# Queries' and keys' stacks of high and low parts: laid out by SBUF-to-SBUF transfers in place of selection products and copies, with the slots of the schedule redone

## What is computed

```python
Q = (x_text @ Wq).reshape(B, T, 4, 32);  K = (x_vision @ Wk).reshape(B, G, 4, 32)
scores = einsum('bthd,bghd->bhtg', Q, K) / sqrt(32)        # masked by vision_mask
topv, topi = top_k(scores, 32);  probs = softmax(topv)
attn_mean = scatter(probs at topi).mean(over heads);  c_t = (attn_mean @ V)
# then: layernorm(x), FiLM by c_t, an S4D filter along T, FiLM, residual, FFN (gelu),
# layernorm, gated residual; a router picks 1 of 8 experts (swiglu) plus a shared expert
```

## Time and profile before

| | us |
|---|---|
| median of 3 runs | 1884.37 (1880.43 to 1888.39) |
| profiled execution | 1881.66 |
| its span on the core | 1879.9 |
| busy in the span: DVE | 1573.5 (84%) |
| PE | 1437.8 (76%) |
| POOL | 1206.7 (64%) |
| ACT | 1112.8 (59%) |
| mean granted TensorE clock | 0.857 of full |

### The profile page before, as it was taken

How to read it: one execution, slowest core, us unless ns; L and a number is a source line. 1 busy time by engine, 2 the same in 40 slices (tenths; PEclk the granted TensorE clock), 3 DMA queues, 4 the chain that set the end, 5 groups by cost and what they waited for, 6 DMA issues and landing times. The chain is left out here.

```text
span 1879.9 us, 21018 instructions
## 1 busy us (share of the span) xinstructions
PE 1437.8 (76%) x6493; PEld 1025.5 (55%) x6493; DVE 1573.5 (84%) x2300; ACT 1112.8 (59%) x2257; POOL 1206.7 (64%) x1325
## 2 busy tenths in 40 slices
PE   4631445767986798779988988897989787887897
PEld 2321324535654565455756565655665666656696
DVE  6899999999999989998999999999999999101321
ACT  3575664476648654865597658765876576233342
POOL 1496873766676657667767875887588747733422
PEclk9665667888897788878999998999989897998999
DMA  7000000000100010002311320122022202652322
GB/s 225 18 4 14 3 16 2 27 12 12 26 25 12 12 40 21 3 12 76 90 51 51 79 79 23 54 76 87 14 54 75 62 13 56 220 161 90 74 48 26
DMA packets 86499, 96.18 MB, mean 51 GB/s; under 512 B 15186, under 2 KB 68186, under 8 KB 86244
## 3 DMA queue, kind: packets, MB, share of 16 engines
q1 hardware_dynamic: 73220, 80.14, 13.7%
q0 software_dynamic: 13168, 14.71, 4.9%
HBM read 75.37 MB, written 19.58 MB: 51 GB/s over the span
## 5 line engine op out<-in xcount | busy, mean ns | idle before, releaser
L1306 DVE MAX8 R<-ZB 128x8 f32<-128x1024 f32 x384 | 470.9, 1226 | 11.8
L1309 DVE MATCH_REPLACE8 ZB<-R,ZB 128x1024 f32<-128x1024 f32 x384 | 464.0, 1208 | 0.0
L653 POOL TENSOR_TENSOR ZB<-ZB 128x1024 f32<-128x1024 f32 x96 | 232.3, 2420 | 146.7 <-ACT ZB L936 135.6
L939 ACT ACTIVATE R<-PS 128x512 f32<-128x512 f32 (+6 forms) x378 | 160.4, 455 | 173.3 <-PE PS L1806 70.8
L655 POOL TENSOR_TENSOR ZB<-ZB 128x1024 f32<-128x1024 f32 x96 | 227.0, 2364 | 7.5
L936 ACT ACTIVATE R<-R 128x32 f32<-128x32 f32 (+3 forms) x352 | 95.0, 271 | 183.5 <-DVE R L1306 132.9
L1298 DVE MAX8 R<-PS 128x8 f32<-128x1024 f32 x128 | 156.4, 1222 | 3.9 <-PE PS L1606 3.9
L1302 DVE MATCH_REPLACE8 ZB<-R,PS 128x1024 f32<-128x1024 f32 x128 | 155.4, 1214 | 0.0
L942 ACT ACTIVATE R<-R 128x1 f32<-128x1 f32 (+1 forms) x384 | 141.6, 391 | 15.2 <-POOL R L640 10.1
L1605 PE MATMUL PS<-ZR 97*128 97x512 f32 x128 | 79.2, 619 | 93.3 <-ACT ZB L936 73.1
L936 ACT ACTIVATE ZB<-ZB,R 128x1024 f32<-128x1024 f32 x128 | 146.3, 1143 | 6.7 <-DVE ZB L1309 6.6
(11 more groups left out here) (246 smaller groups left out, 3321.7 us busy)
## 6 DMA issues: line engine op xcount, KB each, us to landing
ZB<-in_L_ffn_rt_gate SPq DMA_DIRECT2D x21, 512.0 KB, 4.2
ZB<-in_L_ffn_rt_up SPq DMA_DIRECT2D x21, 512.0 KB, 5.4
ZB<-in_L_ffn_rt_down SPq DMA_DIRECT2D x21, 512.0 KB, 6.1
R<-in_x SPq DMA_DIRECT2D x16, 512.0 KB, 3.9
ZB<-in_ctx SPq DMA_DIRECT2D x8, 768.0 KB, 6.5
R<-xs_d SPq DMA_DIRECT2D x39, 128.5 KB, 2.1
out<-R SPq DMA_DIRECT2D x32, 128.0 KB, 2.9
out<-R POOLq DMA_DIRECT2D x32, 128.0 KB, 6.3
```

What stands on the lines that cost most here:

```text
L653: pool.tensor_tensor(e, e, w, ALU.subtract).then_inc(s.g_att, 1)
L939: return act.activation(o, i, ACT.Copy, **k)
L1306: vec.max(ml[:, 8 * r:8 * r + 8], w).then_inc(s.v_tk, 1)
L1309: vec.match_replace(w, ml[:, 8 * r:8 * r + 8], w, NEG).then_inc(s.v_tk, 1)
```

## The change

The selection matrices, their products on PE and the copies on ACT are gone, as are GpSimd's mask transfers. In their place SP issues SBUF-to-SBUF transfers: per batch and head six of 32 x 256 words for the queries (three bands for each of two buffers) and three of 32 x 1024 words for the keys plus the mask row. They read `hl`, so all of `hl` must stay until they have landed: queries' parts are now in its columns 512 to 1023 and the two halves of the keys in 0 to 511 and 512 to 1023; ACT waits for the queries' transfers (qt_in) before it writes the second half, and for the keys' transfers of the batch before (keys_taken) before it writes anything new. The mask is staged in `hl` and not in `acc`. Scores wait for qt_in and k_in. The mask and x are loaded first, ahead of the constants. SP's steps have slot tables of their own (SP_QUERY, SP_KEYS, SP_INPUT, SP_POST, SP_TILE). All slot tables have new values; those that the text speaks of are shown.

```diff
-        sel = alloc_r(576)
...
+            def queries():
+                for b in range(B):
+                    for h in range(H):
+                        yield prep_at(b) + SP_QUERY[h]
+                        on.wait_ge(s.g_lo, 3 * b + 2)
+                        on.wait_ge(s.p_sc, 16 * (b - 1) + 8)
+                        for half in range(2):
+                            q, lo = qt[(2 * b + half) % 3], 512 + 256 * half
+                            for band, part in enumerate((1, 0, 0)):
+                                sp.dma_start(q[32 * band:32 * band + 32, h, :].bitcast(F32),
+                                             hl[32 * h:32 * h + 32, part, lo:lo + 256].bitcast(F32)).then_inc(s.qt_in, 16)
+            def keys():
+                for b in range(B):
+                    for h in range(H):
+                        yield keys_at(b, h) + SP_KEYS[h]
+                        on.wait_ge(s.g_lo, 3 * b + 3)
+                        on.wait_ge(s.mrow_st, 16)
+                        on.wait_ge(s.p_sc, 16 * (b - 1) + 13 + h)
+                        for band, part in enumerate((0, 0, 1)):
+                            sp.dma_start(kt[32 * band:32 * band + 32, h, :].bitcast(F32),
+                                         hl[32 * h:32 * h + 32, part, :].bitcast(F32)).then_inc(s_k[h], 16)
+                        sp.dma_start(kt[96:97, h, :].bitcast(F32), mrow_d[b:b + 1, :]).then_inc(s_k[h], 16)
...
-            def masks():
-                        pool.dma_start(kt[96:97, h, :], mrow_d[b:b + 1, :]).then_inc(s_mask[h], 16)
...
-                    for h in range(H):
-                        yield at + ACT_SEL[h]
-                        own.then_inc(copy(q0[0:96, h, :], bank[0:96, 0:256]))
-                        copy(q1[0:96, h, :], bank[0:96, 256:512]).then_inc(q_sem("prep", b, Q_SEL + h), 1)
+            def keys_taken(b):
+                on.wait_ge(s.mrow_st, 16)
+                for h in range(H):
+                    on.wait_ge(s_k[h], 64 * b)
...
+                        if half:
+                            on.wait_ge(s.qt_in, 384 * (b + 1))
+                        else:
+                            keys_taken(b)
...
-                            copy(kt[0:96, h, half * 512:(half + 1) * 512], q_bank("prep", b, use)[0:96, :]).then_inc(q_sem("prep", b, use), 1)
...
-                def stacked(b, use, h, at_hi, at_lo, lo):
-                        ins = pe.matmul(q_bank("prep", b, use)[0:96, :], sel[:, o:o + 96], hl[:, k, lo:lo + 512], start=k == 0, stop=k == 1)
...
-                    yield max(post_at(b) + 134 + k, tile_slot(j - 1, PE_TILE, T_DOWN) + 2 if j else 0)
+                    yield tile_slot(j, SP_TILE)
...
-DVE_MOMENTS = (55.5, 101.9, 112.7)
+DVE_MOMENTS = (55.8, 99.4, 112.2)
-DVE_ROUTE = (120.4, 123.1)
+DVE_ROUTE = (120.4, 122)
-ACT_KEY = (8.8, 45)
+ACT_KEY = (19.2, 61.1)
-POOL_LOW = (8.7, 9.9, 37.7)
+POOL_LOW = (6.3, 15.2, 62.1)
-POOL_CHUNK = ((-57.6, -8.1, -3.2, 0.5, 4.4), (0.5, ...
+POOL_CHUNK = ((-53.3, -53.3, -53.3, -12.9, -2.1), (-19.4, ...
-DVE_CHUNK = ((-33.2, -10.4), (6.6, 10.3), ...
+DVE_CHUNK = ((-35, -33.6), (-11, -9.9), ...
+SP_QUERY = (28.1, 29.7, 33.4, 34.3)
+SP_KEYS = (8.8, 4.2, 1.9, 0.2)
+SP_TILE = ((-1.9,), (-0.2,), (2.5,), (56.5,), (71.3,))
```

More of the change, by code:

```diff
@@ L94, in keys_at @@
 def keys_at(b, h):
-    return FRAME * b - 31 + 8 * h if b else (-34, -2.5, 5.5, 13.5)[h]
+    return FRAME * b - 31 + 8 * h if b else -34 + 8 * h
 def finish_at(t):
@@ L165 @@
[L165 to L170, removed]
@@ L178 @@
[L178 to L186, removed]
+POOL_FILM_IN = (13.6, 13.6, 13.6, 13.6)
@@ new lines @@
+POOL_FOLD = (13.6,)
+POOL_SPECTRUM = (16.9, 20.9, 23, 23)
+POOL_INV = (25, 31.7)
+POOL_FILM_OUT = (32.3, 34.5, 35, 37)
+POOL_ROOT = (46.3, 99.4, 118.8)
+POOL_RESIDUAL = (46.3, 53.7, 54, 56.5)
+POOL_OUT = (100.6, 101.1, 101.5, 101.5)
+POOL_ROUTE = (124.6, 127.3, 131.5)
+POOL_SH = (134.2, 136.3, 137.7, 139)
+POOL_PREP = (-4.5, 68.5)
+POOL_LOW = (6.3, 15.2, 62.1)
+ACT_FILM_IN = (23.1, 25.2, 29.6, 31.7)
+ACT_INV = (43.5, 46.7)
+ACT_FILM_OUT = (50.8, 52.6, 52.6, 52.6)
+ACT_ROOT = (55, 103.3, 118.2)
@@ new lines @@
+ACT_NORM = (57.8, 120.1)
+ACT_TURN = (61.9, 61.9)
+ACT_UP = (72.4, 72.4, 72.8, 74.8, 82.6, 83.8, 86.5, 87.7)
+ACT_DOWN = (90.7, 91.1, 100.4, 100.4)
+ACT_OUT = (106.2, 106.4, 106.6, 107.2)
+ACT_TURN2 = (122.1, 124.9)
+ACT_ROUTE = (127, 127.2)
+ACT_SILU = (127, 138.3)
+ACT_SH = (139, 139.1, 139.8, 142.3)
+DVE_SPECTRUM = (30.5, 33.3, 34.2, 36)
+DVE_MOMENTS = (55.8, 99.4, 112.2)
+DVE_ROUTE = (120.4, 122)
+DVE_SH = (129.3, 130.9, 131.4, 132.2)
+ACT_PREP = (-0.7, 7.4, 12.4)
+ACT_QUERY = (19.4, 20, 25.8)
@@ L213 @@
     taken_banks[bank] += 1
-NP = 21
 def weave(*parts):
@@ L613, in _ @@
             setup()
-            weave(inputs(), contexts(), kernel_rows(), post(), tiles(), routed())
+            weave(inputs(), contexts(), queries(), keys(), kernel_rows(), post(), tiles(), routed())
         @block.gpsimd
@@ L918, in routed @@
                 pool.drain()
-            weave(attention(), kernel_rows(), prep(), keys(), masks(), weights(), post(), tables(), tiles(), routed())
+            weave(attention(), kernel_rows(), prep(), keys(), weights(), post(), tables(), tiles(), routed())
         @block.scalar
@@ L953, in attention @@
             def attention():
-                yield -70
-                on.wait_ge(s.ld_sel, 16)
-                copy(sel, sel_l).then_inc(s.a_sel, 1)
                 for n in range(16 * B):
@@ L1022, in prep @@
                     on.wait_ge(*q_run("prep", b, QUERY))
[L1023 removed]
+                    keys_taken(b)
+                    own.then_inc(copy(hl[:, 0, 512:1024], bank))
                     copy(tr_prep[:, 0, :], bank).then_inc(q_sem("prep", b, QUERY), 1)
[L1025 to L1032 removed]
+            def keys_taken(b):
+                on.wait_ge(s.mrow_st, 16)
+                for h in range(H):
+                    on.wait_ge(s_k[h], 64 * b)
             def keys():
```

150 lines of the change are left out of this document (48 added, 102 removed).

## The result

The changed kernel takes 1915.52 us (median of four runs, 1905.71 to 1921.42) against 1882.40 (four runs, 1879.94 to 1888.39): ratio 1.0166, 95% interval [1.0108, 1.0224]. It is slower by 33 us; I had forecast 1879 and a range up to 1900. The profiled execution after took 1909.8, its span is 1907.9.

A forecast was written before the change was run, and what follows sets the result against it. VectorE bounds the kernel, busy 1473.91 of 1535 us, with only 30.0 us of waits to win. Sum: 1881.66 - 4.1 + 7.4 - 4.1 + 0 - 1.7 = 1879.2, say 1879; own range 1868 to 1890, overall 1858 to 1900.

The forecast's parts named there:

- So the transfers are covered: cost nothing: Query and key transfers on SP, at 0.42 us an issue, land before ACT's slot 117 and the scores: cost 0.
- the transfers come late (1900): Rival, chance 0.10: SP held past slot 108 or issues of 1.3 us make scores wait in three frames, 21 us.
- The rival with 0.16: PE's clock falls at gate and ranks in six frames, adding 19.0 and 9.8 us: 1904; chance 0.16.
- The ranks, +7.4: DVE reaches the ranks 1.24 us earlier while PE's chain keeps its length, so six frames wait longer: +7.4 us.
- The gate, -4.1: Keys' copies and product gone from between norm and transposes, so DVE's waits for the gate vanish: -4.1 us.
- Scores and POOL, -4.1: Removed work shortens DVE's waits for scores (3.9) and POOL's subtraction (4.3); half of 8.2 us taken: -4.1.
- The preamble, 0: Before tile 0: it begins 6.6 us later, with 6.6 us of chunk 1's work already done; sum 0, -3 to +5.
- The end, -1.7: Last batch alone, 1597 to 1764 us: parts -1.5, -1.3 and +1.1, sum -1.7, from -5 to +2.
- The term -1.5: In the last batch, SP's last tile goes before the stores and its down product no longer holds the transposes: -1.5 us.
- The signs: Expected evidence: DVE busy within 2 us of 1474, no DMA releasing ACT's second-half copy, no end wait for fifth-tile weights.
- theory P: From the experiments, not the prediction: PE's granted clock after its idle stretch sets DVE's gate wait; filling the stretch holds it.

The follow-up runs named there:

- e1: Changed kernel with SP's step of the fifth routed tile moved from slot 71.3 to 91, behind the queries' transfers: 1903.9 us, ratio 1.0084.
- e14: e10 with the last six operations of POOL's table of full tiles at slot 48 and the first add behind the first sum: 1879.1 us, ratio 0.9983.
- e3: Changed kernel with both query halves in one transfer in batches 0, 2, 3, 5, 6: 1892.7 us, ratio 1.0052.
- e12: Changed kernel with ten constant products ahead of PE's turning in batches 0 to 2, SP's fifth tile still ahead of the queries: 1905.5 us, ratio 1.0123.
- e10: e1 with ten constant products ahead of PE's turning in batches 0 to 2: 1884.2 us, ratio 1.0007.
- e13: Kernel before the change with three constant products ahead of PE's turning in batches 0 to 2: 1872.6 us, ratio 0.9942.

## Why the prediction was wrong

**The step that failed: "So the transfers are covered: cost nothing".** SP's block was placed rightly: I had the queries going out "from about slot 104", and they went at 994.35, (994.35 - 838.54)/1.5 = slot 104 of the frame that began at 838.54. Two numbers behind it were wrong. I took 0.42 us for an issue from weight loads; one of the queries' takes 0.68, so 24 need 16.4 us and not 10.1. And I took ACT's slot 117 for the time at which ACT wants to write; a slot only orders ACT's queue. ACT was there at 1003.3, slot 110. They landed just before 1012.1, slot 116, even before "ACT's slot 117", and late all the same. Both errors mattered: at 0.42 each ACT would still have waited some 2.6 us (8.81 - 24 x 0.26).

**That a late transfer costs its whole wait.** This was the rival with chance 0.10, "the transfers come late (1900)", and its estimate, half of 3 x 14 = 21 us, met the measured 21.3. That the number met is luck: no row gave the half, and the 14 us came from an issue of 1.3 us that didn't occur. Its condition was too strict: it asked for SP held past slot 108 or issues of 1.3 us, and 0.68 was enough. The place was another too: not the scores wait but the silu of a routed tile, whose ACT instruction stood behind the copy.

**The clock.** The rival with 0.16 came in part. In e1's trace the gate ran at the lower level in all of frames 1 to 3 and they cost 18 us more than in after's trace, in which none did; the rival's 19.0 was for six frames. It is not a state that the change brings for good: it widens the pause from 3.45 to 10 us, and how soon the clock comes back then differs from run to run. Nor was the kernel before free of it: its gate took 3.55 us in all three frames. The Trainium skill ("TensorE: Matmul & The Clock Gate", Part 1) says that pauses bring the array back to half rate. The traces agree: the turning behind the pause took 1.97 us in after and in e1_down, and 1.10 where the pause was filled.

**The ranks, +7.4: not there.** Waits 14.2 before, 12.9 after. Five of after's seven are 1.07 to 1.11 us, no longer than those of before's last four frames (0 to 1.43); the other two, 4.92 and 2.61, have the first shared product at 3.06 and 3.50 us and not 1.97. So it isn't the shorter stretch of DVE's queue but PE's clock that sets it. **The gate, -4.1: nothing** (4.1 to 4.3; 9.5 at the low clock).

**Scores and POOL, -4.1: the wrong sign.** Scores stayed (3.9 to 4.1), the wait for POOL's sum went from 4.3 to 12.6, and one at the spectrum (L1441) came new with 5.7. The queue lost its mask issues, but the sum's slot had moved from 11.9 to 7.2, close behind POOL's table at slot 5, and I had not written out POOL's queue in the frames that hold one. e14 shows what this was worth: 5 us.

**The preamble, 0: the start was right, the rest not.** The first MAX8 began at 67.7 (forecast 68.7) and chunk 1 was done by then; but frame 0 became 18.5 us shorter, not 6.6. Chunk 1's seven operations took 9.5 us of the preamble, not 6.6; DVE's waits in frame 0 fell from 4.1 to 0.7, and like operations of the other chunks ran shorter, as these of before and after (DVE in frame 0, idle last):

```profile
L1262 DVE TENSOR_SCALAR R<-R 128x512 f32<-128x512 f32 x3 | 5.6, 1876 | 0.0
```

```profile
L1263 DVE TENSOR_SCALAR R<-R 128x512 f32<-128x512 f32 x3 | 3.5, 1174 | 0.0
```

What lengthens them (GpSimd runs beside them in both) was not tried. ACT waited for the queries' transfers here too, 14.3 us before its copy at 50.57; that hardly sets the start, as e3 cut it to 7.7 us and the first MAX8 came at 67.0.

**The end, -1.7: came out +4.0** (302.1 against 298.1 from the last tile's MAX8). 1.9 of it is the first routed product at the lower clock, 5.61 us and not 3.73 as in the kernel before. The term -1.5 had the last pass's down product out of the way of the turning. It still stood ahead of it, at the lower clock, and PE still waited for that tile's weights:

```profile
1736.66 3.81 PE L1896 MATMUL PS<-R,ZB 128*128 128x128 f32 x32 [2.30 <-DMA ZB<-in_L_ffn_rt_up]
1748.57 3.75 PE L1904 MATMUL PS<-ZB,R 128*128 128x256 f32 x8 [8.09 <-issue]
1752.11 1.14 PE L1801 MATMUL PS<-R 128*128 128x128 f32 x8
```

Against the earlier trace rows the down product takes 3.75 us and not 1.97, and the wait is 2.30 and not 3.04: SP's step came ahead of the stores, but it waits for the fourth tile's up product, which ends at 1731.22. The rest stays open; this part lies between 301 and 311 us among the table's runs with the change.

**The signs.** Of what I had named, two things came out against me besides: ACT's copy was released by a DMA in three frames, and PE still waited for the fifth tile's weights in the end. DVE's busy time in its stage was 1454.27 us, 20 under the 1474 that I gave, 14.5 of them in frame 0 (226.39 against 240.93).

**The 33 us.** 21 are the block (e12 against e10). 10 more lie between the medians of after and e12 (1915.5 and 1905.5), by theory P the clock's draw. This part is argued: the two ratios' intervals overlap, and of after's four runs only one of the fast pair has a trace, so that the slow pair, 14 us above, is such a draw is likely but not shown. e10, without the block and with the clock held, stands level with before: 5.5 us later start, -17.1 in frame 0, -11.2 in frames 1 to 3, +14.9 in frames 4 to 6, +3.9 and +3.2 at the end, together -0.8 in the profiled runs, ratio 1.0007. The forecast's sum of -2.5 was near this, but by luck: its terms were not these, and before has the lower clock at its gate. With the clock held at the gate of frames 1 to 3 in both, the change costs: e10 is 11.6 us over e13 (1884.2 against 1872.6, intervals apart), and e14 is still some 7 over it (ratios 0.9983 and 0.9942). The two profiled runs differ by 3.5 us only, 11 more in frames 4 to 6 and 14 less in frame 0, so the traces don't say where all of the 11.6 lies. No run has the new transfers with the old slots, so what the transfers and what the new slots cost is not parted.

## What to carry to other kernels

A slot or a place in a queue is an order, not a time: before a transfer is called covered, find in the trace when the engine that waits for it would really be there, and what stands behind the waiting instruction. Where small transfers replace products, price the issues and not only the bytes, and put them ahead of every step of that queue that waits for another engine's progress. Where work is taken from PE just ahead of products that others wait for, compare the same frames of several traces before a difference is read into an edit; a few constant products, no longer than the pause, were worth more here (9.6 us between medians) than the change (nothing, at its best 0.2%).

## What the runs showed of the hardware that I had not expected

A query transfer from SBUF to SBUF costs SP 0.65 to 0.68 us to issue, for 32 KB as for 64 KB, and one of the keys' (128 KB) 0.59 us (1.78 for three), where a weight load of 512 KB cost 0.37 to 0.42 in the same stretch. After the same pause of some 10 us the granted clock was 0.50 through gate and ranks in one run and 0.76 over the same work in another, worth 6 us a frame. Three products (2.84 us) where the pause had been 3.45 us brought the gate's sixteen products from 3.55 to 1.92 us.
